# Running the expert stage of a routed decoder layer over 71 lots in place of 72

## The reference, cut to what matters

```python
scores = xf @ router_w.T                       # 4096 x 8
top_v, top_i = jax.lax.top_k(scores, 2)
routing_w = jax.nn.softmax(top_v, axis=-1)
out = jnp.zeros_like(xf)
for e in range(8):
    w_e = jnp.sum(jnp.where(top_i == e, routing_w, 0.0), axis=-1)
    h = jax.nn.gelu(xf @ expert_w1[e].T, approximate=False)    # 256 -> 1024
    out = out + h @ expert_w2[e].T * w_e[:, None]              # 1024 -> 256
x = _layernorm(x + out, axis=-1)
```

## Time and profile before

| what | us |
|---|---|
| median of three runs (1202.16 to 1205.75) | 1204.65 |
| the profiled execution: its time | 1203.33 |
| the profiled execution: its span, first to last instruction | 1201.5 |
| of it, from the first transpose of the expert stage to the last add's landing (719.60 to 1166.30) | 446.7 |
| of it, from there to the end | 35.2 |

### The profile page before, as it was taken

One profiled execution on the slowest core, in us unless ns is written; L12 is line 12 of the kernel. 1 busy time (PEld: TensorE's weight loads), 2 busy tenths in 40 slices (PEclk: granted clock), 3 DMA queues, 4 the chain that ended last, 5 costly groups with the idle time before them and its releaser, 6 DMA issues.

```text
span 1201.5 us, 24876 instructions
## 1 busy us (share of the span) xinstructions
PE 942.3 (78%) x8007; PEld 756.7 (63%) x8008; DVE 827.6 (69%) x1264; ACT 460.0 (38%) x1055; POOL 736.1 (61%) x496
## 2 busy tenths in 40 slices
PE   7984098888887887857878429999999999999940
PEld 4542087787787787835656317777777777777730
DVE  4899999999998998327888783444444444444435
ACT  3675223433444443435566312222333233223215
POOL 3575699999999999600000045666666666666522
PEclk9997599999998998979999669999999999999985
DMA  3362102121121221476775402222222222222236
GB/s 100 73 118 52 34 28 67 45 65 57 53 65 48 62 65 44 149 266 195 244 235 202 157 15 45 46 44 44 44 44 44 44 44 44 44 44 44 31 71 231
DMA packets 70136, 100.46 MB, mean 84 GB/s; under 512 B 9312, under 2 KB 51872, under 8 KB 69152
## 3 DMA queue, kind: packets, MB, share of 16 engines
q1 hardware_dynamic: 52816, 76.86, 20.6%
q0 software_dynamic: 16128, 18.93, 10.0%
q10 hardware_dynamic: 1152, 4.19, 0.9%
HBM read 73.96 MB, written 26.38 MB: 84 GB/s over the span
## 4 chain that ended last, share of the span: by engine, by line
PE 44%; POOL 23%; issue 14%; DVE 11%; DMA 4%; ACT 3%; POOLq 0%; SPq 0%; DVEq 0%; ACTq 0%
PE psum L744 17%; POOL mid L1142 13%; PE psum L752 11%; PE psum L754 5%; PE psum L672 3%; PE psum L595 2%; POOL arena L1147 2%; POOL arena L1155 2%; POOL arena L1133 1%; PE psum L736 1%; DMA sum_dram<-arena,mid 1%; PE psum L615 1%; DVE arena L1518 1%; PE psum L646 1%; POOL arena L1149 1%
## 5 line engine op out<-in xcount | busy, mean ns | idle before, releaser
L615 PE MATMUL psum<-consts,mid 128*128 128x128 f32 x2176 | 265.6, 286 | 87.6 <-POOL mid L1142 87.4
L615 PEld LDWEIGHTS psum<-consts,mid 128*128 128x128 f32 x2176 | 260.4, 201 | 99.0 <-issue 52.9
L744 PE MATMUL psum<-arena 128*128 128x128 f16 x3456 | 291.2, 220 | 5.1 <-issue 3.5
L744 PEld LDWEIGHTS psum<-arena 128*128 x3456 | 243.2, 98 | 76.9 <-issue 9.9
L1142 POOL TENSOR_TENSOR mid<-arena 128x2304 f32<-128x2304 f32 (+1 forms) x62 | 250.8, 4067 | 9.8 <-POOL arena L1133 7.6
L752 PE MATMUL psum<-arena 128*128 x576 | 218.1, 380 | 5.1 <-DVE arena L1670 1.2
L1222 POOL DMA_INDIRECT sum_dram<-arena,mid x72 | 142.5, 1980 | 46.1 <-issue 24.7
L1679 DVE SCALAR_TENSOR_TENSOR arena<-psum,arena 128x256 f32<-128x256 f32 x72 | 34.8, 484 | 190.1 <-ACT arena L1041 116.1
L754 PE MATMUL psum<-arena 128*128 x576 | 157.0, 273 | 0.0
L1381 DVE TENSOR_TENSOR mid<-psum,arena 128x4352 f32<-128x4352 f32 x32 | 149.8, 4683 | 0.6 <-issue 0.4
L1388 DVE TENSOR_REDUCE psum<-mid 128x272 f32<-128x4352 f32 x32 | 149.9, 4684 | 0.0
(11 more groups left out here) (191 smaller groups left out, 1400.2 us busy)
## 6 DMA issues: line engine op xcount, KB each, us to landing
arena<-w_t SPq DMA_DIRECT2D x64, 256.0 KB, 2.8
arena<-w_t SPq DMA_DIRECT2D x16, 1024.0 KB, 10.4
arena<-x SPq DMA_DIRECT2D x32, 128.0 KB, 2.1
arena<-x_dram SPq DMA_DIRECT2D x8, 512.0 KB, 5.5
arena<-ctx_t SPq DMA_DIRECT2D x8, 512.0 KB, 6.3
arena<-ctx SPq DMA_DIRECT2D x8, 512.0 KB, 7.1
x_dram<-mid SPq DMA_DIRECT2D x8, 512.0 KB, 3.3
arena<-sum_dram SPq DMA_DIRECT2D x8, 512.0 KB, 4.9
```

The costliest lines, as they stand in the source:

```text
L615: last = nc.tensor.matmul(psum[:, u, c * P:(c + 1) * P], products[half][:, w, c * P:(c + 1) * P], ident, start=(a + w == 0 and c == 0), st ...
L744: last = nc.tensor.matmul(dst, block_of(w, e, 0, c * F + j * P, P), x[:, u, c * P:(c + 1) * P], start=(k == 0 and c == 0), stop=(k == 2 an ...
```

## The change

The expert stage runs `LOTS` = 71 lots. The tables of the routing keep their 72 columns; the last column is no longer used. PE's, ACT's and DVE's loops end one group earlier (groups 2 to 16, lots 8 to 67). Lots 68, 69 and 70 are written out behind the loops, with the same steps as in the body. PE's `load_word` now stands ahead of lot 68 and there is none behind it. The three closing `products` carry the numbers 71, 72 and 73. POOL's written-out stream has one `fetch_rows`, one `fetch_gates` and one `send` less, and SP waits for 71 adds.

```diff
+LOTS = (TOP * T + N_EXP * (P - 1)) // P
...
-            sp.wait_ge(y_added, 16 * SLOTS)
+            sp.wait_ge(y_added, 16 * LOTS)
...
             four_lots(0)
             four_lots(1)
-            with pe.Fori(2, SLOTS // 4) as i:
+            with pe.Fori(2, LOTS // 4) as i:
                 four_lots(i)
-            word = load_word(SLOTS // 2 - 1)
-            products(SLOTS, 0, expert(word, 1), expert(word, -1))
-            products(SLOTS + 1, 1, None, expert(word, 0))
-            products(SLOTS + 2, 0, None, expert(word, 1))
+            last = LOTS // 4
+            word = load_word(2 * last + 1)
+            for v in range(3):
+                s = 4 * last + v
+                transpose_rows(s, v, last)
+                products(s, v % 2, expert(word, v - 3), expert(word, v - 5))
+            products(LOTS, 1, expert(word, 0), expert(word, -2))
+            products(LOTS + 1, 0, None, expert(word, -1))
+            products(LOTS + 2, 1, None, expert(word, 0))
...
-            quads(act, SLOTS, lot, 8)
-            result_beside(SLOTS - 3, 1, SLOTS // 4 - 1)
-            gelu(SLOTS - 1, 1)
-            result_beside(SLOTS - 2, 2, SLOTS // 4 - 1)
-            result_beside(SLOTS - 1, 3, SLOTS // 4 - 1)
+            quads(act, LOTS // 4 * 4, lot, 8)
+            for v in range(3):
+                lot(4 * (LOTS // 4) + v, v, LOTS // 4)
+            result_beside(LOTS - 3, 0, LOTS // 4)
+            gelu(LOTS - 1, 0)
+            result_beside(LOTS - 2, 1, LOTS // 4)
+            result_beside(LOTS - 1, 2, LOTS // 4)
...
-            for s in range(SLOTS + 8):
-                if s < SLOTS:
+            for s in range(LOTS + 8):
+                if s < LOTS:
                     fetch_rows(s, s % 4)
                 if s >= 8:
                     send(s - 8, s % 4)
-                if 4 <= s < SLOTS + 4:
+                if 4 <= s < LOTS + 4:
                     fetch_gates(s - 4, s % 4)
...
-            quads(dve, SLOTS, lot, 8)
-            result_out(SLOTS - 3, 1, SLOTS // 4 - 1)
-            split_hidden(SLOTS - 1, 1)
-            result_out(SLOTS - 2, 2, SLOTS // 4 - 1)
-            result_out(SLOTS - 1, 3, SLOTS // 4 - 1)
+            quads(dve, LOTS // 4 * 4, lot, 8)
+            for v in range(3):
+                lot(4 * (LOTS // 4) + v, v, LOTS // 4)
+            result_out(LOTS - 3, 0, LOTS // 4)
+            split_hidden(LOTS - 1, 0)
+            result_out(LOTS - 2, 1, LOTS // 4)
+            result_out(LOTS - 1, 2, LOTS // 4)
```

## The result

The kernel with 71 lots takes 1196.69 us (median of four runs, 1196.09 to 1197.52) against 1205.2 us before: a ratio of 0.9934, 95% interval 0.9915 to 0.9953. A later measurement of the same two kernels gave 0.9930 (0.9916 to 0.9944). That is 8.0 to 8.4 us less. The forecast was 6.4 us less (1198.2 us): the time is inside its range, and the gain is about 2 us more than forecast. The first interval (5.7 to 10.2 us less) still contains the forecast of 6.4; the second (6.7 to 10.1) just does not. The profiled execution took 1196.53 us with a span of 1194.7 us, 6.8 less than the span before.

A forecast was written before the change was run, and what follows sets the result against it. PE was taken to bound the expert stage, with a chain of adds at its end. Terms -6.30 - 0.40 + 0.06 + 0.25 gave -6.4 us, from 1204.65 to 1198.2 us (ratio 0.9947), range 1194.5 to 1202.

The forecast's parts named there:

- What bounds the stage: Expert stage: the chain runs through PE, matmuls hold 94% of the stretch shown, a looped lot takes 5.98 us.
- Rival A: Expert stage: the adds set the pace, not PE; one add less saves 4.6 to 5.65 us, 1199.5 us; 10%.
- One lot's products and transposes, -6.30: PE, lots 68 to 71: one interval falls away with the 0.63 us gap ahead of products(72), saving 6.30 us.
- The first closing product, -0.40: PE's tail: products(71) takes 5.35 us where products(72) took 5.75, saving 0.4, bounds 0 and 0.58.
- Leaving the loop ahead of lot 68, +0.06: PE ahead of lot 68: loop exit plus load_word (0.63) costs 0.06 us more than loop-back plus load_word (0.57).
- Three lots in straight code, +0.25: PE, three lots written out behind the loop: cost between -0.1 and +0.6 us, taken as +0.25.
- The chain of adds, 0: Last three adds: 13.8 us from first send to last landing as before, gaps 0.71 and 1.83, bounds -1.1 to +1.1.
- rival B: Last adds: the 1.83 us gap becomes 0.71, all else as summed, -7.5 us, 1197.1 us; 13%.
- ACT, DVE, POOL: Other engines: idle time covers ACT's and DVE's lots out of the loop; POOL's dropped gathers and send are worth 0.
- The last stage: After the last add's landing: 35.2 us of norms and stores follow unchanged, 0, loads and stores differing by +-0.5.
- Rival C: Most is given back: first-pass price, no products(71) gain, second long gap; -4.0, 1200.6 us, measured gain under 3.6; 10%.

The follow-up runs named there:

- 68 lots: The kernel before with 68 lots in place of 72, all in loops, nothing written out; ratio 0.9785, 25.9 us less.
- the move out of the loops: The kernel before, all 72 lots, with PE's, ACT's and DVE's loops ending at lot 67 and lots 68 to 71 written out; ratio 0.9994.
- The straight kernel: The changed kernel (71 lots) with PE's 17 groups all written out, no loop on PE, ACT and DVE keeping theirs; 1187.86 us, ratio 0.9868.
- kernels of 72 lots: The kernel before, that kernel with lots 68 to 71 written out (ratio 0.9994), and that kernel without a loop on PE (1194.16 us, 0.9927).

## Why the prediction was right, and where it was short

**What bounds the stage: right.** PE sets the pace. Four lots less in the loop take exactly their 23.9 us off PE's timeline, and the time follows (68 lots). Rival A falls.

**One lot's products and transposes, -6.30: right.** It is one interval plus the 0.63 gap. Putting the load_word back restores a gap, 0.89 in all. The gap was laid to leaving the loop and the load_word together; the move out of the loops shows that it is the load_word's alone.

**The first closing product, -0.40: half.** products(71) took 1144.82 - 1139.28 = 5.54 where I took 5.35. The gain is 0.21; why not more is open.

**Leaving the loop ahead of lot 68, +0.06: the step that failed in sign.** I compared the 0.57 ahead of lot 68 with the 0.63 ahead of products(72) as if both gaps ended at the same kind of instruction. The one ends at transposes, which don't need the word; the other at L744, which does. With the transposes behind the exit the gap was 0.21, so the term is -0.36. The move alone has 0.44.

**Three lots in straight code, +0.25: mis-sized.** Lots 68 and 69 took 6.17 and 5.79 where the rows before had 6.32 and 5.83, and lot 70 5.64 (1133.64 to 1139.28) against 5.55: -0.10 in all. I read 23.76 for lots 4 to 7 as straight code in full and so saw only 0.16 between straight and loop. The row held the entry to the loop. The straight kernel has 23.4, and 0.5 per group. And I charged the new code with a share of the 0.78 of the loop's first pass. The same lots read for the first time in straight code took 23.51 in place of 24.70, so that price belongs to the loop and not to fresh code.

Together the last three make 0.58 (-0.19 + 0.42 + 0.35), the difference between 6.39 and PE's 6.97.

**The chain of adds, 0: rival B came true, as a fixed property and not a chance.** I took the 1.83 as it stood and gave 13% to its going; no row before told that it belongs to send 71. It stands ahead of send 71 in all three kernels of 72 lots whose waits were left as they are, and a kernel of 71 lots has no send 71. That is 1.1 of the 1.25 gained; the rest is shorter landings.

**ACT, DVE, POOL: right at 0.** products(73) waits 1.16 us for DVE as products(74) did, and the results are ahead of their sends. **The last stage: right**, 35.65 against 35.2.

With -6.97 and -1.25 the sum is -8.2, and the two measurements say 8.0 and 8.4. That is the best case of the prediction's own sum (-8.0), or just past it, and far from its middle: the range held the time at its edge. The sum was too tight where it gave one term, the leaving of the loop, no bounds at all. Rival C, a gain under 3.6 us, falls: the intervals begin at 5.7 and 6.7.

## What to carry to other kernels

A unit of padded work that is taken away is worth its own interval plus the overheads that happen to sit beside it; here a load_word (0.89), a trip round the loop (0.44) and one late send (1.1) made about 8 us out of a lot of 5.55. When two gaps are compared, look at which instruction each one ends at and what that instruction needs. Before a stretch is used as the price of straight code, see whether a loop's entry or exit lies inside it; a loop of four lots on the engine that sets the pace cost as much in branches as the whole change gained.

## What the runs showed of the hardware

Going round PE's loop costs 0.4 to 0.5 us each time, though no page of code is read while it runs; written out, the stage reads a page about every 9 us (36 in 310 us), and its groups of four stay at 23.4 to 23.5 us. A load of one value into PE's registers cost 0.89 us in front of a product without transposes; moved from the front of each group into the middle of the products ahead, it left four lots at 23.41 us against 23.45. Between the landing of an add in HBM and the send that waited for it lie 0.71 us at the end of the stage, but 1.83 ahead of send 71 (in three of three kernels of 72 lots whose counts were left alone). Ahead of send 51 there are 1.71 (in the kernel before). With `y_added` raised by 96 beforehand both were gone. Why is open: the value waited for is not shown to be the cause, since send 45, which then waited for 816, had no such delay.
